# Splitting the bfloat16 pass of every expert product into two products of 256 columns

## The reference, cut to what matters

```
gate_v, gate_o = top-2 gates of x            # (tokens, heads, experts), six of eight are zero
xv  = x @ v_w[h, e]                          # 64 products of 128x128x128 for a batch
v   = sum over e of gate_v * xv
att = softmax(q k^T * SCALE);  ctx = att @ v
out = sum over h, e of gate_o * (ctx @ o_w[h, e])   # 64 more
```

## Time and profile before

| what | before |
|---|---|
| time, median of 3 executions | 1483.1 us (1482.65 to 1484.07) |
| span of the profiled execution, first to last instruction | 1482.2 us |
| TensorE busy (PE) | 1419.3 us, 96% |
| weight loads (PEld) | 961.5 us, 65% |
| VectorE / ScalarE / GpSimd busy | 89% / 86% / 58% |
| bfloat16 pass of the expert products | 1024 products, 390 ns recorded for each |

### The profile page before, as it was taken

The page is one execution under the profiler, slowest core; times in us unless marked ns, Lnnn a source line. Parts: engine busy times, 40 slices in busy tenths (PEclk is TensorE's granted clock), DMA queues, the critical chain, the costliest instruction groups (busy, mean ns, idle before and its releaser), DMA issues.

```text
span 1482.2 us, 34265 instructions
## 1 busy us (share of the span) xinstructions
PE 1419.3 (96%) x9905; PEld 961.5 (65%) x9905; DVE 1323.1 (89%) x4498; ACT 1276.0 (86%) x4428; POOL 858.9 (58%) x1345
## 2 busy tenths in 40 slices
PE   4678999999999999999999999999999999999998
PEld 2355666666666666666666666666666666666654
DVE  3677999999999999999999999999999999999986
ACT  3657888999988899998889999888899988889886
POOL 3112656566565666656566666656556565655667
PEclk8589999999999999999999999999999999999999
DMA  5420000000000000000000000000000000000000
GB/s 135 138 56 16 8 16 16 14 15 12 16 8 16 16 14 15 13 16 9 16 16 15 15 13 16 9 16 16 15 14 13 15 9 16 14 15 7 8 3 4
DMA packets 68954, 30.13 MB, mean 20 GB/s; under 512 B 19168, under 2 KB 68768, under 8 KB 68768
## 3 DMA queue, kind: packets, MB, share of 16 engines
q1 hardware_dynamic: 51552, 19.31, 4.9%
q10 hardware_dynamic: 17216, 8.65, 2.1%
HBM read 17.31 MB, written 2.10 MB: 13 GB/s over the span
## 4 chain that ended last, share of the span: by engine, by line
PE 89%; DVE 3%; POOL 2%; ACT 2%; issue 2%; DMA 1%; SPq 1%; POOLq 0%; DVEq 0%
PE psC L308 58%; PE psA L308 13%; PE psB L308 7%; PE psB L532 4%; PE psC L628 2%; PE psA L420 1%; PE psB L552 1%; PE psA L465 1%; POOL TE L3428 1%; POOL accO L3440 1%; ACT PTB L1343 1%; DVE TE L2500 1%; POOL v_sb L3433 0%; SPq L3811 0%; DVE nmA L2239 0%
## 5 line engine op out<-in xcount | busy, mean ns | idle before, releaser
L3440 POOL TENSOR_TENSOR accO<-accO,TE 128x512 f32<-128x512 f32 x192 | 246.4, 1283 | 147.1 <-DVE TE L2500 140.9
L1343 ACT ACTIVATE TE<-psC,gateO 128x128 f32<-128x128 f32 x1024 | 292.6, 375 | 24.6 <-PE psC L308 16.4
L1343 ACT ACTIVATE TE<-psC,gate 128x128 f32<-128x128 f32 x1024 | 297.0, 394 | 17.7 <-PE psC L308 10.4
L2500 DVE SCALAR_TENSOR_TENSOR TE<-psC,gate,TE 128x128 f32<-128x128 f32 x1024 | 284.7, 340 | 29.1 <-PE psC L308 19.4
L2500 DVE SCALAR_TENSOR_TENSOR TE<-psC,gateO,TE 128x128 f32<-128x128 f32 x1024 | 287.2, 342 | 12.5 <-PE psC L308 8.0
L3428 POOL TENSOR_TENSOR TE<-TE 128x256 f32<-128x256 f32 x256 | 192.1, 751 | 164.2 <-DVE TE L2500 159.4
L308 PE MATMUL psC<-Vh,xTh 128*128 128x512 f32 x512 | 264.6, 517 | 2.2 <-ACT PS L1343 1.2
L308 PE MATMUL psC<-Oh,ch 128*128 128x512 f32 x512 | 262.4, 513 | 0.7 <-DVE TE L2500 0.6
L308 PE MATMUL psC<-Oh,cl 128*128 128x512 f32 x512 | 203.1, 397 | 0.0
L308 PE MATMUL psC<-Vh,xTl 128*128 128x512 f32 x512 | 202.7, 396 | 0.0
L308 PE MATMUL psC<-Vl,xTb 128*128 128x512 bf16 x512 | 199.9, 390 | 0.0
(11 more groups left out here) (228 smaller groups left out, 3449.4 us busy)
## 6 DMA issues: line engine op xcount, KB each, us to landing
bdB<-Kc SPq DMA_DIRECT2D x384, 16.0 KB
raw<-in_L_ffn_v_w ACTq DMA_DIRECT2D x8, 512.0 KB, 4.4
raw<-in_L_ffn_o_w ACTq DMA_DIRECT2D x8, 512.0 KB, 4.0
x_sb<-in_x SPq DMA_DIRECT2D x32, 64.0 KB, 2.1
ctx_sb<-in_ctx SPq DMA_DIRECT2D x32, 64.0 KB, 2.0
bdA<-Kc SPq DMA_DIRECT2D x128, 8.0 KB
Qb<-Qc SPq DMA_DIRECT2D x128, 8.0 KB
bias_sb<-in_mask_Bx1xSxS_ff SPq DMA_DIRECT2D x32, 64.0 KB, 2.0
```

What stands on the lines that cost most here:

```text
L1343: return A.activation(o, i, func, **kw)
L2500: m = V.scalar_tensor_tensor(TE[:, i, e], psC[:, p, e * P:(e + 1) * P], gates[:, e:e + 1], TE[:, i, e], ALU.mult, ALU.add)
L3440: G.tensor_tensor(accO[:], TE[:, slot(b, H1)] if h == 1 else accO[:], TE[:, slot(b, H1 + h)], ALU.add).then_inc(o_fe, 1)
```

## The change

The third pass of `experts` is issued as two products, columns 0 to 255 and columns 256 to 511 of the same bank, each against the same stationary operand `low`. The first has neither the start nor the stop flag, the second has the stop flag and the semaphore increment. The two four-byte passes stay at 512 columns.

```diff
@@ -636,7 +636,8 @@
                 pe.wait_ge(*free[half])
                 mm(o, hi, wh, True, False)
                 mm(o, lo, wh, False, False)
-                mm(o, low, wl, False, True).then_inc(done, 1)
+                mm(o[:, 0:256], low, wl[:, 0:256], False, False)
+                mm(o[:, 256:512], low, wl[:, 256:512], False, True).then_inc(done, 1)
```

## The result

| | before | after |
|---|---|---|
| median of 20 executions each | 1484.01 us (1482.3 to 1487.35) | 1486.76 us (1484.2 to 1488.89) |
| ratio, 95% interval | | 1.0017 [1.0011, 1.0023] |
| the same pair again, 13 and 9 executions | 1483.95 us | 1486.91 us, 1.0022 [1.0012, 1.0032] |
| span of the profiled execution | 1482.2 us | 1486.4 us |

The kernel became slower by 2.75 us, and by 2.96 us when it was timed again; these are differences of medians, and the ratios say 2.5 us (interval 1.6 to 3.4) and 3.3 us (1.8 to 4.7). The forecast was +3.7 us, to 1486.8 us. That the time agrees within 0.1 us is luck: the kernel before, timed beside it, came out 0.9 us above the three executions from which the forecast started. The difference lies inside the second interval and just above the first.

The account below looks back on a forecast made before the run. The prediction took TensorE's products to bound the kernel: 0.97 x (2.7 us of seams + 1.1 us of loads behind the halves) = 3.7 us, so 1483.1 + 3.7 = 1486.8 us. Its 8-in-10 range was 1483.3 to 1491.5 us.

Parts of the forecast that it names:

- The time is the sum of TensorE's steps.: Whole run: time is what TensorE's products hold each other up for; what is added to one is added to the time.
- The cost of a low pass is 227 ns: Low pass before the change: 213 ns of columns, some 3 of seam, some 11 of its own weight load not hidden.
- Term 1: Between the two halves of the low pass: a seam of 2.6 ns, second load hidden; 1024 times, 2.7 us.
- Term 2: Behind the second half: the next four-byte load needs about 110 ns beside 109; 1.1 ns on the mean, 1.1 us.
- 0.97 of it counts: All 1024 low passes: 832 mid-run count in full, the other 192, near start and end, by 0.85.
- The second load: Rival at the second half: its bfloat16 load shows, seam 13.6 ns, 14.6 us more, 1497.7 us; chance 0.12.
- The straight line: Skill's load-and-product figures at 256 columns: two halves 65 ns over one whole, some 65 us; only part of the 0.12 rival.
- The shorter rhythm: Rival in the expert passes: most products hand over 9 to 10 ns sooner, -5.7 us, 1477.4 us; chance 0.08.
- The absorbed case: Rival: TensorE's waits too short to show take out the halves' cost, no change, 1483.1 to 1484.5 us; chance 0.10.

Follow-up runs that it names:

- kernel 7: Against the kernel before: low pass kept whole at 512 columns and issued first of the three passes; 1466.3 us against 1484.3, ratio 0.9880.
- kernel 8: Against the kernel before: low pass whole, first in half 0 and last in half 1; 1477.7 us against 1484.3, ratio 0.9956.
- kernel 6: Against the kernel before: low pass cut into four parts of 64 columns, then one of 256; 1493.3 us against 1484.3, ratio 1.0059.
- kernel 3: Against the kernel before: low pass cut into 128 columns, then 384 (128 + 384); 1485.7 us against 1483.5, ratio 1.0014.
- kernel 2: Against the kernel before: low pass cut into 384 columns, then 128; 1517.9 us against 1483.5, ratio 1.0229.
- kernel 5: Against the kernel before: low pass cut into 320 columns, then 192; 1500.8 us against 1484.3, ratio 1.0111.
- kernel 4: Against the kernel before: low pass whole, float32r remainder pass cut into 256 + 256; 1484.1 us against 1483.5, ratio 1.0002.

## Why the prediction was right

Point by point, as the prediction put it:

1. *The time is the sum of TensorE's steps.* Right for the change: a batch went from 43.10 to 43.22 us, no wait was added to the list, VectorE's work is unchanged, and outside the expert products and their followers the steps didn't grow (about 1 us less over 32 batches). As a general statement it is too strong, and its proof was weaker than it looks. The list of waits and the rhythm of the earlier trace rows miss waits that a modelled end covers: behind `psA<-ident_b,atb` the high pass ended after 479 ns before, where 286 is usual, once a batch. Kernels 7 and 8 met such a wait and lost 4.5 and 5.5 us to it.
2. *The cost of a low pass is 227 ns, 11 of them its own load.* Right in kind, and a little more in size: where its load is hidden (kernel 7) it steps 216 ns from end to end, and 231 behind a float32r pass, 15 ns apart.
3. *Term 1, the seam, 2.6 ns.* A little less: between the ends of the halves lie 109 ns, as forecast, but of the whole pass 128 + 384 takes 2.1 ns from its neighbours (the table: 484 x 2 + 240 x 2 + 156 x 3 + 111 x 2 + 29 x 2 over 1024). Timed, it is 2.0 ns a seam (kernel 6), and 2.2 us for one seam in each of 1024 passes (kernel 3, interval 0.9 to 3.4). These intervals don't tell 2.1 from 2.6.
4. *Term 2, the load behind the half, 1.1 ns on the mean.* The medians have the change 1, 0, 3 and 0 ns over 128 + 384 for float32r, transposition, plain and bfloat16 followers, 1.0 ns on the mean (484 x 1 + 156 x 3 + 29 x 2 over 1024). By the means of the steps, in which the short steps of the high pass count, it is 1.4 to 1.7 ns, with 2.2 to 2.7 for float32r followers in place of the forecast 0.7. That the total came near is in part luck: transpositions, put at 2.2 ns, cost nothing, and float32r and plain followers cost more. That the load is what counts here, kernels 2 and 5 show, where it is 32 and 14 us over the one seam.
5. *0.97 of it counts.* 3.2 us of steps gave 2.75 and 2.96. With tens of us it is less, 0.75 to 0.86.
6. *The rivals.* The second load never showed, not even beside 27 ns. The straight line through the figures of the Trainium skill, "TensorE: Matmul & The Clock Gate", section "Back-to-back issue gap", had 98 ns for a half and 131 for a whole; the halves step 109 ns, quarters 56, and a whole 216 to 231, so the trace doesn't agree with it. The shorter rhythm didn't spread: the step from high to remainder pass is 235 ns at the median before and after, the remainder pass handed over within 0.23 us in 84 of 1024 cases before and in 40 after, and the short steps of the high pass behind a low pass nearly vanished. The absorbed case would have given 1.4 us at most; the intervals begin at 1.6 and 1.8.

The forecast of +3.7 us was 0.7 to 1.0 too high against the medians. By the median steps, term 1 is 0.5 ns a product too large and term 2 right, 3.1 ns in place of 3.7. But the records don't agree to better than 1 us: the usual batch is 0.12 us longer, 3.8 us over 32; the steps sum to 3.2 us by medians and 4.3 to 4.5 by means; the timings say 2.75 and 2.96. The interval of the first timing holds 3.2 and not 3.8, that of the second holds both. One execution's span says nothing at this size: the two profiled executions of the change have spans of 1486.4 and 1484.7 us.

## What to carry to other kernels

Where TensorE sets the time, ask what follows a product before cutting it. A seam costs 2 to 3 ns here; a part shorter than the load of the next stationary operand costs the difference each time, so a short part belongs first. The same view, the loads' starts beside the products' starts, shows loads that aren't hidden today: putting the bfloat16 pass ahead of the four-byte passes was worth six times what the cut cost. And when TensorE gets faster, look for waits in the steps between ends, at the first product of each group, and not only in the list of waits: kernel 8 lost a third of its gain in one such place.

## What the runs showed of the hardware

- A float32r product of 512 columns steps 235 ns from end to end and two of 256 step 117 each (kernel 4), a bfloat16 one of 256 columns 109, at the same granted clock of 1.00: 0.46 and 0.42 ns a column.
- A 128x128 bfloat16 load hides beside 27 ns of bfloat16 columns (kernel 6), and not behind a float32r pass, where it starts with its own pass and shows with 15 ns. Kernel 7 shows it hidden behind short bfloat16, short plain four-byte products and transpositions (216 ns steps from all three), and kernel 8 behind a bfloat16 pass of 512 columns (216 ns in 217 places), so it isn't the length of the pass ahead that matters. Why float32r does, no run shows.
- A four-byte load needs 110 ns before a float32r or plain product and clearly less before a transposition, which loses 9 ns behind a part of 53 ns (350 against 341) where the others lose 57 to 59 (kernel 2).
